# Clipping y on GpSimd, three normalised tiles on VectorE, and another order of every engine's step

## The reference

```
x = x + conv(layernorm over channels of x)
   conv: f = Wf x, v = Wv x (384 channels, 8 heads of 48), images folded into 4 quarters of 28x28;
         16 pooled centers per quarter and head; cosine of every token with every center;
         sigmoid; only the largest center of a token is kept; weighted sum back, projection Wp
t = t + ffn(layernorm over channels of t)
   ffn: _bitlinear(W1) -> gelu -> _bitlinear(W2), weights replaced by their signs
   _quantize_activations_groupwise(y), for 5 groups of 6 images:
       gamma = max |y of the group|
       xq    = clip(y * 128 / (gamma + 1e-5), -128 + 1e-5, 128 - 1e-5)
   images 30 and 31 belong to no group: their ffn output stays 0
```

## Time and profile before

| | us |
|---|---|
| median of 3 runs | 3082.18 (3080.43 to 3089.51) |
| profiled execution, its own time | 3084.92 |
| its span | 3083.0 |
| PE busy | 2921.4 (95%) |
| DVE busy | 2716.7 (88%) |
| ACT busy | 2181.7 (71%) |
| POOL busy | 1879.6 (61%) |

### The profile page before, as it was taken

The page is one execution under the profiler, slowest core; times in us unless marked ns, Lnnn a source line. Parts: engine busy times, 40 slices in busy tenths (PEclk is TensorE's granted clock), DMA queues, the critical chain, the costliest instruction groups (busy, mean ns, idle before and its releaser), DMA issues.

```text
span 3083.0 us, 63330 instructions
## 1 busy us (share of the span) xinstructions
PE 2921.4 (95%) x20790; PEld 2025.7 (66%) x20790; DVE 2716.7 (88%) x5906; ACT 2181.7 (71%) x4510; POOL 1879.6 (61%) x4658
## 2 busy tenths in 40 slices
PE   3999999999999999999999999999999999999984
PEld 2677777557777765677776667777755777776552
DVE  3788888889999989899998989999989999998975
ACT  1677767887777779677676977776788777777941
POOL 1577766437777753777776357777744777775342
PEclk9999999999999999999999999999999999999987
DMA  1011111002222210222221012222100222221024
GB/s 50 17 40 33 33 33 33 9 17 64 64 64 65 72 39 1 67 72 69 64 64 48 1 48 64 64 64 64 56 25 17 64 64 67 72 68 33 5 83 133
DMA packets 30939, 154.80 MB, mean 50 GB/s; under 512 B 6483, under 2 KB 6676, under 8 KB 30612
## 3 DMA queue, kind: packets, MB, share of 16 engines
q1 hardware_dynamic: 30612, 150.74, 17.5%
HBM read 76.06 MB, written 74.66 MB: 49 GB/s over the span
## 4 chain that ended last, share of the span: by engine, by line
POOL 44%; PE 32%; issue 17%; DVE 3%; ACT 2%; DMA 0%; POOLq 0%; SPq 0%; DVEq 0%
PE ps L1016 9%; PE ps L1065 8%; PE ps L941 5%; POOL eq L434 5%; POOL mo_x L387 5%; POOL mo_t L387 4%; POOL nxy L416 3%; POOL ninv L421 3%; POOL mo_x L380 3%; POOL ny L414 3%; POOL nxy L418 2%; POOL cinv L428 2%; PE ps L905 2%; POOL mo_t L372 1%; POOL n2c L402 1%
## 5 line engine op out<-in xcount | busy, mean ns | idle before, releaser
L941 PE MATMUL ps<-wfT,xn 97*112 97x384 f32 x1792 | 729.9, 515 | 3.4 <-DVE cosb L691 2.8
L1016 PE MATMUL ps<-tok,w1T 98*128 98x392 f16 x2880 | 615.1, 337 | 1.6 <-ACT turns L564 1.6
L505 ACT ACTIVATE sq<-ps 112x384 f32<-112x384 f32 x896 | 432.4, 490 | 212.9 <-PE ps L941 209.8
L757 DVE TENSOR_REDUCE hmax<-ps 128x1 f32<-128x392 f32 x720 | 393.7, 561 | 61.0 <-PE ps L1016 49.1
L1016 PEld LDWEIGHTS ps<-tok,w1T 98*128 98x128 f16 x2880 | 284.6, 99 | 203.9 <-issue 48.6
L941 PEld LDWEIGHTS ps<-wfT,xn 97*112 97x112 f32 x1792 | 275.9, 181 | 191.6 <-issue 54.4
L681 DVE TENSOR_REDUCE n<-sq 112x32 f32<-112x1536 f32 (+1 forms) x256 | 394.3, 1540 | 7.1 <-ACT sq L505 3.9
L561 ACT ACTIVATE turns<-ps,scale 128x1176 f32<-128x1176 f32 x240 | 367.9, 1533 | 43.0 <-DVE scale L777 38.7
L448 POOL CAST turns<-turns 128x392 f16<-128x392 f32 x240 | 169.3, 706 | 353.5 <-ACT turns L561 352.0
L472 ACT ACTIVATE xnT<-ps,mo_x 112x96 f32<-112x96 f32 x896 | 304.1, 447 | 68.8 <-POOL mo_x L389 68.8
L832 DVE SCALAR_TENSOR_TENSOR turns<-turns 128x1176 f16<-128x1176 f32 x240 | 333.5, 1390 | 0.0
(11 more groups left out here) (136 smaller groups left out, 6339.5 us busy)
## 6 DMA issues: line engine op xcount, KB each, us to landing
xbuf<-in_x SPq DMA_DIRECT2D x64, 588.0 KB, 4.7
out<-xbuf SPq DMA_DIRECT2D x64, 588.0 KB, 6.0
turns<-out SPq DMA_DIRECT2D x60, 588.0 KB, 6.3
out<-turns SPq DMA_DIRECT2D x60, 588.0 KB, 4.4
cst<-in_constants SPq DMA_DIRECT2D x1, 644.0 KB
tok<-in_L_ffn_W SPq DMA_DIRECT2D x2, 142.5 KB
wf<-in_L_conv_Wf SPq DMA_DIRECT2D x1, 144.0 KB
tok<-in_L_conv_Wv SPq DMA_DIRECT2D x1, 144.0 KB
```

The lines of the kernel that those rows point to most:

```text
L505: nc.scalar.activation(sq[:, t, :], bank(2 + t % 2, TN, D), ACT.Square).then_inc(f_sq, 1)
L757: v.tensor_reduce(o, bank(6 + u % 2, 128, HT), AX.X, ALU.max, apply_absolute_value=True)\
L941: mm(bank(2 + t % 2, TN, D), xn[:, k % 2, t * TN:(t + 1) * TN], wfT[:, :], start=True, stop=True)\
L1016: ins = mm(dst, w1T[:, c * 128:(c + 1) * 128], tok[:, bass.ds(place, 1), part, s * HT:(s + 1) * HT].rearrange("p a n -> p (a n)"), start=p ...
```

## The change

Each y is no longer scaled and clipped from above on DVE. Instead two bounds are made once per group from `gamma + 1e-5` (`bound`, two tiny DVE instructions), POOL clips y in place between them with one `tensor_scalar` of min and max, and DVE's last instruction on y multiplies by the scale and adds t. Three of the seven tiles of t are normalised on DVE (`normalise_rest`, L749 of the changed kernel) instead of ACT. And the lists of all four engines stand in another order. The core of the diff:

```diff
@@ GpSimd
-            attention = [(X, 1, moments("x", EPS_C)), (M, 1, norm_guess), (M, 1, newton(0)), (M, 1, newton(1)),
-                         (M, 1, newton(2)), (X, 1, center_squares), (X, 1, center_norms), (A, 0, marks),
-                         (R, 0, moments("t", EPS_T), FFN)]
+            def clipped(g, part):
+
+                def step(k, q, place, use):
+                    if isinstance(place, int) and place == 0:
+                        pool.wait_ge(g_bound, 2 * g)
+                    for d in range(3 * place, 3 * place + 3) if part == "last" else (place,):
+                        y = y32[0:C, bass.ds(d, 1), :].rearrange("c a n -> c (a n)")
+                        nc.gpsimd.tensor_scalar(y, y, bound[0:C, 0:1], bound[0:C, 1:2], ALU.min, ALU.max)\
+                            .then_inc(S["y_clip"], 1)
+                return step
+
+            def attention(g, part):
+                return [(R, 1, moments("t", EPS_T), FFN), (X, 1, moments("x", EPS_C)), (M, 1, norm_guess),
+                        (M, 1, newton(0)), (M, 1, newton(1)), (M, 1, newton(2)), (R, 0, clipped(g, part), FINAL),
+                        (X, 1, center_squares), (A, 0, marks), (X, 1, center_norms)]
@@ ScalarE
-                return [(R, 1, normalise("t", 6, 1), FFN), (A, 1, copy_sim(0)), (R, 1, n_high(0, part), FFN),
...
+                return [(R, 1, n_high(1, part), FFN), (A, 1, copy_sim(1)), (X, 1, normalise("x", 0, 0)),
...
@@ VectorE
+            def normalise_rest(k, q, place, use):
+                done(dve, "t_shift", q)
+                done(dve, "n_ps", q - 2)
+                m = mo["t"][:, k % 2, :, :]
+                for t in range(TA, T):
+                    ins = v.tensor_scalar(nT[:, k % 2, t, 0:C], bank(7, TN, C, (t - TA) * C), m[:, 8, t:t + 1], m[:, 9, t:t + 1],
+                                          ALU.mult, ALU.add)
+                ins.then_inc(S["t_norm"], 1)
...
                 v.tensor_scalar(scale[:, i:i + 1], den[:, i, 1:2], QB, None, ALU.mult).then_inc(g_scale, 1)
+                if i == 1:
+                    v.tensor_scalar(bound[:, 0:1], den[:, i, 0:1], QCLIP / QB, None, ALU.mult).then_inc(g_bound, 1)
+                    v.tensor_scalar(bound[:, 1:2], den[:, i, 0:1], -QCLIP / QB, None, ALU.mult).then_inc(g_bound, 1)
...
-            def scaled(g, part):
-                def step(k, q, place, use):
-                    if isinstance(place, int) and place == 0:
-                        dve.wait_ge(g_scale, 2 * g)
-                    for d in range(3 * place, 3 * place + 3) if part == "last" else (place,):
-                        v.tensor_scalar(y_of(d), y_of(d), scale[0:C, 1:2], QCLIP, ALU.mult, ALU.min)\
-                            .then_inc(S["c_min"], 1)
-                return step
...
-                    done(dve, "c_min", q - GQ)
+                    done(dve, "y_clip", q - GQ)
                     t = fin[:, k // 2 % 2, k % 2 * QN:(k % 2 + 1) * QN]
-                    v.scalar_tensor_tensor(t, y_of(place), -QCLIP, t, ALU.max, ALU.add).then_inc(S["final"], 1)
+                    v.scalar_tensor_tensor(t, y_of(place), scale[0:C, 1:2], t, ALU.mult, ALU.add).then_inc(S["final"], 1)
...
-                         (A, 0, maxima), (X, 1, q_scaled), (R, 0, stats("t", 6), FFN),
...
+                        (R, 0, stats("t", 6), FFN), (X, 1, center_floor), (X, 1, q_scaled), (X, 1, q_placed),
+                        (M, 0, norms(0, TA)), (R, 0, finish(part), FINAL), (X, 0, stats("x", 0)), (A, 0, masked),
+                        (R, 0, normalise_rest, FFN), (M, 0, norms(TA, T)), (R, 0, n_low(0), FFN)]
@@ TensorE
...
+                        (A, 1, spread(0)), (A, 1, spread(1)), (X, 1, centers), (R, 1, hidden_tiles(5, 6), FFN),
+                        (M, 0, features(0, 1)), (M, 0, features(1, 2)), (R, 0, to_tokens("t", 6, g), FFN),
+                        (X, 1, center_products), (M, 0, features(2, 4)), (M, 0, features(4, 6)), (X, 1, q_back),
...
```

More of the change, by code:

```diff
@@ L122, in build @@
         scale = sb("scale", [128, 2])
+        bound = sb("bound", [128, 2])
         turns = sb("turns", [128, 11 * FC * HT // 2])
@@ L191, in build @@
         f_out = [sem(f"f_out{i}") for i in range(2)]
[L192 removed]
+        g_max, g_T, g_row, g_all, g_eps, g_rec, g_scale, g_bound = (sem(n) for n in ("g_max", "g_T", "g_row", "g_all", "g_eps", "g_rec", "g_scale", "g_bound"))
         w_loaded, pe_set, dve_set, pool_set = sem("w_loaded"), sem("pe_set"), sem("dve_set"), sem("pool_set")
@@ L435, in marks @@
                     .then_inc(S["eq_done"], 1)
-            attention = [(X, 1, moments("x", EPS_C)), (M, 1, norm_guess), (M, 1, newton(0)), (M, 1, newton(1)),
-                         (M, 1, newton(2)), (X, 1, center_squares), (X, 1, center_norms), (A, 0, marks),
-                         (R, 0, moments("t", EPS_T), FFN)]
+            def clipped(g, part):
[11 more added lines that the diff above has]
+                        (X, 1, center_squares), (A, 0, marks), (X, 1, center_norms)]
             def group(g, part):
-                pipeline(pool, g, part, attention)
+                pipeline(pool, g, part, attention(g, part))
                 def middle_chunk(k, i, place):
@@ L454, in _ @@
                 group(g, "middle")
-            pipeline(pool, GROUPS, "last", attention)
+            pipeline(pool, GROUPS, "last", attention(GROUPS, "last"))
         @block.scalar
@@ L805, in attention @@
             def attention(g, part):
[L806 to L810, removed]
-                         (A, 0, maxima), (X, 1, q_scaled), (R, 0, stats("t", 6), FFN),
-                         (R, 0, scaled(g, part), FINAL), (X, 1, q_placed), (M, 0, norms(0, TA)),
-                         (X, 0, stats("x", 0)), (A, 0, masked), (R, 0, finish(part), FINAL)]
+                return [(R, 1, n_low(1), FFN), (A, 1, summed), (R, 1, h_largest(0, 2), FFN), (A, 1, denominators),
+                        (A, 1, factors), (A, 1, first_heads), (R, 1, h_largest(2, 3), FFN), (A, 1, second_heads),
+                        (R, 1, h_largest(3, 5), FFN), (X, 1, pooled), (M, 1, cosine), (A, 1, residual(0)),
+                        (R, 1, h_largest(5, 6), FFN), (X, 1, centers), (A, 1, residual(1)), (A, 0, maxima),
+                        (R, 0, stats("t", 6), FFN), (X, 1, center_floor), (X, 1, q_scaled), (X, 1, q_placed),
+                        (M, 0, norms(0, TA)), (R, 0, finish(part), FINAL), (X, 0, stats("x", 0)), (A, 0, masked),
+                        (R, 0, normalise_rest, FFN), (M, 0, norms(TA, T)), (R, 0, n_low(0), FFN)]
             def group(g, part):
@@ L1031, in attention @@
             def attention(g):
[L1032 to L1038, removed]
-                        (M, 0, features(6, 7)), (A, 0, find_first)]
+                return [(R, 1, hidden_tiles(0, 2), FFN), (A, 1, project), (X, 1, x_back(0)),
+                        (R, 1, hidden_tiles(2, 4), FFN), (X, 1, x_back(1)), (R, 1, hidden_tiles(4, 5), FFN),
+                        (A, 1, spread(0)), (A, 1, spread(1)), (X, 1, centers), (R, 1, hidden_tiles(5, 6), FFN),
+                        (M, 0, features(0, 1)), (M, 0, features(1, 2)), (R, 0, to_tokens("t", 6, g), FFN),
+                        (X, 1, center_products), (M, 0, features(2, 4)), (M, 0, features(4, 6)), (X, 1, q_back),
+                        (A, 0, marks_back), (X, 0, to_tokens("x", 0)), (M, 0, features(6, 7)), (A, 0, find_first),
+                        (M, 0, scores), (A, 0, sim_back(0)), (R, 0, t_back(0), FFN), (A, 0, sim_back(1)),
+                        (R, 0, t_back(1), FFN), (A, 0, aggregate)]
             def column_to_row(n, i):
```

10 lines of the change are left out of this document (5 added, 5 removed).

## The result

The changed kernel takes 3243.1 us (median of 4 runs, 3229.68 to 3244.3) against 3083.07 for the kernel before (median of 4): ratio 1.0503, 95% interval 1.0482 to 1.0524. It is slower, by 160 us. The forecast was 3219 in a range of 3165 to 3275; 3243 lies outside 3200 to 3232, which the prediction gave to its own path.

What follows compares the result with a forecast made beforehand. Bound: POOL's loop, then `cosb` and `top`, 18.74 us a slot. Adding 120 us in 96 middle slots, 16 in group 1 and 1 for the bounds gave +137 on 3084.92: 3222, median 3219, range 3165 to 3275.

Steps and rivals of the forecast that it cites:

- its own path: The walked slot of the new order, middle period 19.8 to 20.1 us, total 3200 to 3232, given 0.45.
- The new wait ahead of `qT`: On DVE, `qT` waits 1.27 us for `cinv`, now behind `eq` on POOL; DVE's queue stands behind it.
- The path from there to the next `cosb`: Late x's statistics on DVE delay POOL's `mo_x` and Newton part; period 19.99, given as 20.0 against 18.74 us.
- `Q` at 7.0: On DVE, `Q` comes 7.0 us behind `cosb`, after PE's transposition, which has two more feature tiles ahead of it.
- The hold of the finishing: DVE's last instruction on y may wait for POOL's power in `mo_t`: 0 to 0.3 us, 0.13 taken.
- The rival of the full hold: On DVE, the finishing waits until POOL's power ends: period 20.18 us, 18 us more, 3237; chance 0.27.
- The collisions that go: DVE and POOL no longer hold each other at L788/`mo_t` (0.33) and L798/L380 (0.64): 0.97 us relieved per slot.
- The clip: On POOL between `ninv` and `csq`: 1.4 us taken, free in a room of 3.6 us.
- The upper bound from L402: POOL's clip priced per element from a max on 56 elements: 3.5 us for 784, twice that for both bounds.
- The three tiles at nothing: Three tiles of t on DVE behind `sim`, 0.9 us together, beside POOL's 8.7 us: costed at nothing.
- The changes of group: Second passes untouched; the two bounds cost about 0.2 us five times, 1 us.

Runs made afterwards that it cites:

- e7: The changed kernel's order of all four lists with the work of the kernel before (y scaled on DVE, all seven tiles on ACT): 3244.22 us, ratio 1.0504.
- e12: Kernel before with clip on POOL, three tiles on DVE, finishing ahead of x's statistics, plus late `cinv`, `cn`, `qT` and `qT`'s transposition: 3215.56 us, ratio 1.0424.
- e5: Kernel before with the clip on POOL and the finishing of y behind the second part of the squared norms: 3085.31 us, ratio 0.9988.
- e11: Kernel before with the clip on POOL and the finishing of y ahead of x's statistics, all seven tiles on ACT: 3064.70 us, ratio 0.9921.
- e2: Kernel before with only three of t's tiles normalised on DVE instead of ACT: 3090.55 us, ratio 1.0018.
- e9: Kernel before with the clip on POOL and the finishing of y between t's statistics and `Q`, where L788 stood: 3099.81 us, ratio 1.0040.
- e3: Kernel before, in its old order, with both the clip on POOL and three of t's tiles on DVE: 3087.71 us, ratio 1.0011.
- e10: Kernel before with the clip on POOL, the finishing between t's statistics and `Q`, and three of t's tiles on DVE: 3068.15 us, ratio 0.9927.
- e1: Kernel before, in its old order, with only the clip on POOL and the scale put into the finishing of y: 3089.31 us, ratio 1.0018.
- e4: Changed kernel with the finishing of y moved behind the three normalised tiles instead of ahead of x's statistics: 3232.45 us, ratio 1.0476.

## Why the prediction was right, and where its numbers were off

- **The new wait ahead of `qT`.** Right. Walked: `cinv` ends 6.13 behind `cosb`, `qT` at 6.22 after 1.27 of waiting. Measured: 6.13 (840.71 + 0.56 - 835.14), 6.17 and 1.14. e7 shows it without the work, e12 without the other moves.
- **The path from there to the next `cosb`.** Right. Statistics of x end at 11.04 (walked 11.10), `mo_x` starts at 11.12 (11.18), the period of such a slot is 19.92 (19.99). PE idles 0.87 ahead of `sim`'s transpositions, a little under the microsecond that was said.
- **`Q` at 7.0.** This is the term that was too small. It held for every second slot (6.99); in the others PE brings the transposition 0.36 later and `Q` comes at 7.28. The prediction looked only at what stands between features and transposition, not at the transpositions of t ahead of the products, which can now wait for DVE. The mean period was 20.07, 128 us over 96 slots instead of 120; group 1 had 19.14 instead of 18.98. `Q` waits 0.44 to 0.73 for PE, where some 0.3 was said.
- **The hold of the finishing, 0 to 0.32, taken 0.13.** There was none: 1.02 inside the power in the changed kernel, e5 and e11. The 0.06 over the old 0.96 is there wherever the finishing has its new form, and gone in e2 and e7, which keep the old one. The rival of the full hold (period 20.18, 3237) is near in time and wrong in mechanism. By the Trainium skill, "SBUF — State Buffer", section "Who interferes with whom", an instruction of VectorE with two SBUF inputs would have waited for a GpSimd instruction that reads SBUF and started first, until its end. For the power the rows of e5 and e11 contradict that, and the measurement decides; for `eq` e9 agrees with it to 0.2 us. Why the power doesn't hold is not shown; the prediction's guess, that seven elements are read early, was not tested.
- **The collisions that go.** Right in size: `mo_t`'s first is back at 0.21. A new one came that I hadn't seen: L390 takes 0.68 instead of 0.21 in the slot shown, since it starts inside the finishing. It costs nothing, for `mo_x` waits 1.17 behind it; the prediction, without this collision, said about 1.5.
- **The clip.** Right that it is free, 0.99 us in a room of 3.6. The upper bound from L402 was far off. It took the step from 0.21 us for 7 elements to 0.42 for 56 as a price per element, but L419 of the changed kernel, another `tensor_scalar` on 56 elements, takes 0.24.
- **The three tiles at nothing.** Right, 0.94 for three, by e2 and e3.
- **The changes of group.** Costed at 1 us, measured +16: the term that was mis-sized most. By the traces 11 of them lie between a group's last `eq` and the second pass, while the pipeline's last slots still have the longer path, 1 in the five second passes and 4 from there to the next group's first `eq`. That the longer path makes the 11 is not shown step by step. e12's stretches grew by 9 us in all.

Sum: 158 on the span against 137. Of the 21 that were missing, 15 are at the changes of group and 7 in group 1, 2 in the last eight quarters, less 3 that start and end gave back. The middle groups came out at 121 against 120, though by 92 intervals of 1.31 instead of 96 of 1.25. That this term fits so well is partly luck: the walk had a hold of 0.13 that wasn't there, and lacked the alternation's 0.14.

## What to carry to other kernels

On an in-order engine a short operation is only as early as what stands ahead of it: a 0.56 us power put behind a 1.71 us subtraction left another engine idle for 1.14 us in each slot, with all of that engine's queue behind the wait. Here work that went to an engine with idle time cost at most 0.3% and earned nothing either, except where it took a wait off the loop (e10), so walk one slot from the closing instruction to itself, before and after, with the lists of every engine on the way, PE's too. And before an instruction on two SBUF inputs is moved, look at what starts beside it and at who waits for its end.

## What the runs showed of the hardware

- A POOL instruction that starts behind the finishing (DVE, two SBUF inputs, 96x784) is held until some 0.15 us before the finishing's recorded end, and then takes its own time: L381 lasts 1.01 (0.22 elsewhere), the power 2.27 (1.49), L373 0.94 (0.21). That is so in e1, e3, e4 and e9.
- The other way round it depends on POOL's instruction. Started inside `eq` (two inputs, 112x896) with 0.40 or 1.59 us of it still to come, the finishing takes 1.23 or 2.42 (e9); started inside the clip with 0.91 to come, 1.74 (e1, at 3053.06). Less its own 1.02 that is a hold until 0.19 us before POOL's recorded end each time, for all that was left. Started inside a power of 7 elements it takes its usual 1.02, with 1.17 of the power to come (e5).
- POOL's clip, `tensor_scalar` with min and max against two pointers, takes 0.99 us for 784 elements of 96 partitions, 1.3 ns per element.
- The `scalar_tensor_tensor` of 784 elements takes 1.02 us with the scale by a pointer, multiply and add, where it took 0.96 with an immediate, maximum and add. No run separates the pointer from the operation.
